# A graph attention layer on one core: own attention moved ahead of the heads, its addresses computed at the top of PE's body

## The reference

```
ft = (feat @ W).reshape(n, 8, 32)
a1 = einsum('nhd,hd->nh', ft, attn_l);  a2 = einsum('nhd,hd->nh', ft, attn_r)
e  = leaky_relu(a1[src] + a2[dst], 0.2)
m  = segment_max(e, dst);  ex = exp(e - m[dst]);  s = segment_sum(ex, dst)
out = segment_sum(ft[src] * (ex / s[dst])[:, :, None], dst);  elu(out)
```

## Time and profile before

| | us |
|---|---|
| median of 3 runs | 10875.36 (10864.18 to 10881.65) |
| profiled execution | 10858.35 |
| its span | 10856.6 |
| PE busy | 6806.7 (63%) |
| DVE busy | 5031.4 (46%) |
| POOL busy | 5048.3 (46%) |
| ACT busy | 1617.7 (15%) |

### The profile page before, as it was taken

How to read it: one execution, slowest core, us unless ns; L and a number is a source line. 1 busy time by engine, 2 the same in 40 slices (tenths; PEclk the granted TensorE clock), 3 DMA queues, 4 the chain that set the end, 5 groups by cost and what they waited for, 6 DMA issues and landing times. The chain is left out here.

```text
span 10856.6 us, 124953 instructions
## 1 busy us (share of the span) xinstructions
PE 6806.7 (63%) x23840; PEld 4761.3 (44%) x23841; DVE 5031.4 (46%) x16052; ACT 1617.7 (15%) x3209; POOL 5048.3 (46%) x5307
## 2 busy tenths in 40 slices
PE   5565555555554444444579997566666666640999
PEld 3453333343443333333345554444444444430666
DVE  7834444334333333333321221377777777776111
ACT  0010000000000000000222222222222222222222
POOL 0027777777557777777200000266666666630000
PEclk6555555555555555555567776666676776765999
DMA  1111111111110000000000002244444444421000
GB/s 39 48 21 26 26 26 26 26 26 26 21 16 13 13 13 13 13 13 13 5 6 0 0 0 72 74 115 114 115 114 115 114 114 115 114 82 35 16 15 16
DMA packets 352968, 481.08 MB, mean 44 GB/s; under 512 B 147816, under 2 KB 253262, under 8 KB 352750
## 3 DMA queue, kind: packets, MB, share of 16 engines
q0 software_dynamic: 198016, 334.70, 13.0%
q1 hardware_dynamic: 154734, 144.44, 4.3%
HBM read 429.61 MB, written 49.16 MB: 44 GB/s over the span
## 5 line engine op out<-in xcount | busy, mean ns | idle before, releaser
L554 POOL DMA_INDIRECT conv_rows<-table,conv_idx x3520 | 3346.6, 951 | 1850.2 <-issue 1072.0
L628 PE MATMUL conv_pm<-conv_rows,conv_sel 128*128 128x64 f32 (+1 forms) x7040 | 2283.2, 423 | 2177.1 <-DMA conv_rows<-table,conv_idx 2177.0
L628 PEld LDWEIGHTS conv_pm<-conv_rows,conv_sel 128*128 128x128 f32 x7040 | 1762.3, 311 | 2698.0 <-DMA conv_rows<-table,conv_idx 1384.9
L1288 POOL DMA_INDIRECT att_rows<-ft_rows,att_idx x1760 | 1684.7, 957 | 2697.4 <-ACT att_idx L1302 2197.2
L616 DVE TENSOR_TENSOR acc<-acc,conv_pm 128x64 f32 (+1 forms) x3520 | 719.4, 204 | 2303.1 <-PE conv_pm L628 1521.5
L1432 PE MATMUL att_pm<-att_rows,att_sel 128*128 128x264 f32 x3520 | 1465.9, 582 | 218.5 <-DVE sums L1578 111.4
L600 DVE TENSOR_SCALAR conv_sel<-iota,edges,edge_w 128x128 f32<-128x128 f32 x3528 | 995.4, 362 | 444.6 <-issue 413.4
L1432 PEld LDWEIGHTS att_pm<-att_rows,att_sel 128*128 128x128 f32 x3520 | 956.0, 289 | 520.3 <-DVE sums L1578 177.7
L1578 DVE TENSOR_TENSOR sums<-sums,att_pm 128x264 f32 x1760 | 752.7, 428 | 384.5 <-PE att_pm L1432 310.2
L544 ACT ACTIVATE conv_idx<-edges 128x8 int32 x440 | 91.7, 209 | 4305.2 <-PE conv_pm L628 4253.9
L1548 DVE TENSOR_TENSOR att_rows<-att_rows,att_pwi 128x1056 f32<-128x1056 f32 x440 | 547.1, 1244 | 123.6 <-issue 75.8
(11 more groups left out here) (304 smaller groups left out, 6654.4 us busy)
## 6 DMA issues: line engine op xcount, KB each, us to landing
conv_rows<-table,conv_idx POOLq DMA_INDIRECT x3520, 2.4
att_bc<-places SPq DMA_DIRECT2D x110, 512.0 KB, 3.7
att_rows<-ft_rows,att_idx POOLq DMA_INDIRECT x1760
ft_rows<-proj_ft SPq DMA_DIRECT2D x25, 544.0 KB, 3.0
x_spilled<-x_rows SPq DMA_DIRECT2D x1, 12800.0 KB, 39.8
elu_xg<-x_spilled SPq DMA_DIRECT2D x25, 512.0 KB
x_rows<-x SPq DMA_DIRECT2D x6, 2048.0 KB, 18.8
out<-ffn_y SPq DMA_DIRECT2D x24, 512.0 KB, 2.9
```

Of the source, the lines that this page charges most:

```text
L554: pool.indirect_dma_start(out=dest(k), out_offset=None, in_=table, in_offset=bass.IndirectOffsetOnAxis(ap=idx[:, k:k + 1], axis=0)).then_i ...
L628: ins = nc.tensor.matmul(pm[q % RING][:, i, :], sel[:, (q % RING) * QUAD + i, :], rows[:, k, :], start=True, stop=True)
L1288: pool.indirect_dma_start(out=rows[:, k, :], out_offset=None, in_=K.ftd, in_offset=bass.IndirectOffsetOnAxis(ap=idx[:, k:k + 1], axis=0)). ...
```

## The change

PE's part of own attention is split in two. `own_places` loads a quad's word and makes its four addresses; `own_attention` waits once and then issues all 16 matmuls. Three quads' addresses are made at the top of the body, the fourth's between the sums of quads 0 and 1. Own attention now comes in one piece directly after the sums of quad 1, ahead of the heads. The row ends stand between the second and the third step of quad 2's sums. On ACT the second refill changes places with `columns`. The first block, ahead of the loop, is handled by the same functions in the same order as before.

```diff
@@ ACT, body
                     ends(n)
                     carries(n)
                     weights(n)
-                    if not isinstance(b, int) or b + 2 < NB:
-                        columns(b + 2, (i + 2) % PERIOD)
                 refill(1)
+                if more and (not isinstance(b, int) or b + 2 < NB):
+                    columns(b + 2, (i + 2) % PERIOD)
@@ PE
-            def own_attention(n, q):
+            def own_places(n, q):
 
                 at = [a2b[:, ds(w, 1), :, :].rearrange("p a c h -> p (a c h)")
                       for w in quad_windows(pe, K, n * NQ + q)]
                 for a in at:
                     pe.lower_ap(a)
-                if q == 0:
-                    pe.wait_ge(t_ready, n + 1)
-                    pe.wait_ge(a2_kept, n + 1)
-                    gate(pe, passed)
-                for k in range(QUAD):
-                    s = q * QUAD + k
-                    ins = mm(pa[:, s * PARTS * HEADS:(s + 1) * PARTS * HEADS], sel_t[:, s, :], at[k], start=True,
+                return at
+
+            def own_attention(n, at):
+
+                pe.wait_ge(t_ready, n + 1)
+                pe.wait_ge(a2_kept, n + 1)
+                gate(pe, passed)
+                for s in range(SEGS):
+                    ins = mm(pa[:, s * PARTS * HEADS:(s + 1) * PARTS * HEADS], sel_t[:, s, :], at[s], start=True,
                              stop=True)
-                if q == NQ - 1:
-                    ins.then_inc(a_done, 1)
+                ins.then_inc(a_done, 1)
@@ PE, ahead of the loop
-            for q in range(NQ):
-                own_attention(0, q)
+            own_attention(0, [a for q in range(NQ) for a in own_places(0, q)])
@@ PE, body
                 n = b + 1
+                at = []
+                if more:
+                    for q in range(NQ - 1):
+                        at += own_places(n, q)
                 factor(b)
                 sums(b, i, 0)
+                if more:
+                    at += own_places(n, NQ - 1)
                 sums(b, i, 1)
                 if more:
+                    own_attention(n, at)
                     heads_turned(n)
-                    own_attention(n, 0)
-                    own_attention(n, 1)
+                sums(b, i, 2, 0, 2)
+                if more:
                     ends_turned(n)
-                    own_attention(n, 2)
-                    own_attention(n, 3)
-                sums(b, i, 2)
+                sums(b, i, 2, 2, QUAD)
                 if more:
                     carries_turned(n)
                 sums(b, i, 3, 0, 2)
```

## The result

| | before | after |
|---|---|---|
| median us | 10878.51 (4 runs, 10864.18 to 10887.69) | 10803.76 (4 runs, 10783.12 to 10809.18) |
| ratio | 1 | 0.9929, 95% interval 0.9912 to 0.9946 |
| profiled execution | 10858.35 | 10783.12 |
| its span | 10856.6 | 10781.4 |
| attention, first to last block's first weighing | 2656.3 (24.37 a block) | 2571.2 (23.59 a block) |

The kernel is 0.7% faster; 10801 was forecast. The stage gave 85 us in the profiled execution, where 74 were forecast; the rest of the program took 10 us back, which is inside the scatter of the runs.

What follows compares the result with a forecast made beforehand. No engine is full; a block was taken to run mostly on DVE's clock. (0.35 + 0.33) x 109 = 74 us off the profiled 10858.35 gives 10784, stated as 10801 us on the timed runs' basis, range 10770 to 10835.

Steps and rivals of the forecast that it cites:

- DVE's clock: Attention stage: a block mostly runs on DVE's time, busy 78% and idle 5.5 us a block.
- a label that was not to be believed: The view's 310.2 us of DVE adds waiting for PE were doubted; much was said to be DVE's own address work.
- The 1.59 us: DVE's gap before the third quad's adds: claimed to be DVE's own address work and to stay.
- Own attention in one piece: PE's 16 matmuls together: removes DVE's wait before the reduction of a2, 0.35 us a block, bounds 0.27 and 0.40.
- Fourth add: Third quad's adds on DVE: the fourth no longer waits, as its sums are split around the row ends; 0.33 us a block.
- Address work at the top, hidden: PE's three quads of addresses, 4.1 us, delay the factor 0.8 to 0.9 us; cost 0, upper bound 0.5 a block.
- Rival 3: PE's address work at the body's top delays the first sums 1.7 us: +45 us, 10920; chance 0.09.
- ACT's refill: ACT's refill ahead of the columns: gain 0; DVE's loop-closing stall may grow 0 to 0.5 us each, taken as 0.
- rival 2: Gain taken back by a longer DVE stall at the loop's closing or late row ends: 10860 to 10880; chance 0.13.
- Sum: Attention stage: (0.35 + 0.33) us a block x 109 = 74 us gained.

Runs made afterwards that it cites:

- 9: Changed kernel with ACT's second refill behind the columns again, plus DVE's third-quad addresses made ahead of the scan over the rows: 10634.13 us, 0.9785.
- Experiment 12: Kernel before, PE and ACT untouched, with DVE's third-quad addresses made ahead of the scan over the rows: 10879.24 us against 10880.14, 0.9999.
- experiment 2: Kernel before with only PE's addresses hoisted (three quads to the body's top, the fourth between sums of quads 0 and 1): 10803.55 us, 0.9941.
- 11: Changed kernel with ACT's second refill behind the columns again and the row ends ahead of all the third quad's sums: 10783.94 us, 0.9927.
- Experiment 4: Changed kernel with the fourth quad's PE addresses made at the top of the body too: 10819.7 us, 0.9953.
- 10: Changed kernel, ACT's old order, DVE's third and last quads' addresses ahead, PE's quads one at top, two behind first sums, one behind second: 10581.3 us, 0.9738.
- experiment 6: Changed kernel, ACT's old order, DVE's third-quad addresses ahead of the scan over the rows, run on the slow chip: 13064.2 us, 0.9898.
- experiment 5: Changed kernel, ACT's old order, row ends ahead of all the third quad's sums, run on the slow chip: 13098.35 us, 0.9923.

## Why the prediction was right

*DVE's clock, and a label that was not to be believed.* Right. The 1.59 us stayed (1.58) although PE's products were now early, and fell to 0.22 when DVE's own address work was moved (9). One detail was wrong: I expected the label to stay "waits for PE"; it turned into "issue" as soon as PE's products were early. I also took PE to be out of this gap altogether. Experiment 12 shows that it was close behind: with DVE's address work gone from there, the first add of an ordinary block starts 0.87 us earlier and not 1.36, the second 0.46, and the fourth not at all.

*Own attention in one piece, 0.35 us a block.* Measured over 102 blocks the gap ahead of the reduction went from 0.31 to -0.09: 0.40, the upper bound. The size is right, the name is not: in experiment 2 own attention is in two pieces at its old place, and the gap is gone as well.

*Fourth add, 0.33 us.* From 2.16 to 1.82 us for the four: 0.34. But I put it down to the split around the row ends, and experiments 2 and 11 show that the hoisting gives it.

*Address work at the top, hidden.* The factor came 0.68 to 1.14 us late, by the block's position in the loop, where 0.8 to 0.9 was forecast; the first sums stayed at 1.39 us after the weighing, and went from 1.39 to 1.63 in loop-closing blocks, where DVE is later still. Experiment 4 shows how thin the cover is: one quad more costs 0.34 us a block. That speaks against reading the Trainium skill ("Advanced Engine Details and Errata", Sequencer and Instruction Queues) so that address work would run on past a waiting matmul. Rival 3 had the right mechanism but the wrong place (row ends, not the first quad's adds).

*ACT's refill, gain 0, stall 0 to 0.5 us longer per closing.* Measured 0.27 to 0.29 us, 0.09 a block. The stall's growth is what is true of rival 2; how much of it is the refill's, experiments 2 and 11 leave open.

*Sum.* 0.40 + 0.34 - 0.09 = 0.65; 0.78 was measured. Of the missing 0.13, 0.06 is the scan over the rows, which before came 1.73 us after the end of DVE's own row scans and now 1.67; why, no experiment tells. The rest is spread in steps below 0.05 and not resolved. That the timed medians fell by 75 us, against 74 forecast, is in part luck: the stage gave 85.

## What to carry to other kernels

When a view says that an engine waits for another, compare the end of what it is said to wait for with its start: where they lie far apart (1.5 us here), look at the engine's own register work between them; it can be put under an operation that is already queued. If two engines compute addresses for the same stretch, hoist both: hoisting only the reader's gave 0.0% (12), only the producer's 0.6% (2), both, with the new order and the last two groups of DVE's, 2.6% (10). Work hoisted to the top of a loop body is free only as far as the next waiting instruction reaches, so spread it over several such stretches.

## What the runs showed of the hardware that was not expected

- One chip of the four in the experiments ran all five kernels timed on it more than 20% slower (the kernel before took 13195 us there, 10864 to 10880 on the other three), with 34 us for an attention block where three of the same kernels took 21.7 to 23.6 on another chip. DVE's own operations kept their lengths there (the weighing 1.25 us, an add 0.43); waits between engines grew, DVE's for the heads up to 12 us. The gain of 1.4 us a block that experiment 6's kernel has over experiment 5's on another chip (9 against 11) shrank to 0.3.
- A matmul whose semaphore is not yet there holds back the register work behind it on PE, and does so in all 109 blocks of the trace of before (experiment 4).
- DVE stalls 2.2 to 2.5 us at each closing of the loop. In the trace of before, DVE's next record comes 2.7 to 3.1 us behind its branch in all 34 closings, and in each of these gaps lies one transfer of the queue of instructions, of 0.3 to 0.55 us, begun 0.9 to 1.3 us behind the branch. So the engine most likely waits for its own code; what fills the rest of the gap no record shows. The Trainium skill ("Runtime: NRT & Kernel Launch", Instruction fetch mechanics) tells of a fetch at a taken branch whose target has left the instruction memory, and gives PE four times the room; PE, whose loop closes after the same three blocks, goes on 0.06 us behind its branch at all 34 closings, which agrees.
